# Writing an attention mask into the score banks from ScalarE instead of TensorE, in a kernel of attention and mixture of experts on one core

## The reference

```python
# layer 0: attention, 16 heads of 64, one key and value head for all
q = l2norm(ln(x) @ Wq) * q_scale ; k = l2norm(kv[..., :64]) * k_scale   # a null key and value in front
sim = einsum('bhid,bjd->bhij', q, k) * 8 + attn_bias                   # bias from relative positions
sim = where(causal, neg, sim)
sim = where(mask, sim, neg)                                            # mask: (16, 256), one bool per key
x = x + ln(einsum('bhij,bjd->bhid', softmax(sim), v) @ Wout) * g_out
# layer 1: router with top 2 of 8 experts, two shared experts, leaky gates
y = sum over chosen experts of weight * (leaky(x @ w_gate) * (x @ w_up)) @ w_down
x = x + y + shared experts
```

## Time and profile before

| | before |
|---|---|
| median of 3 executions | 1048.13 us (1047.93 to 1050.3) |
| profiled execution, its own time | 1048.86 us |
| its span (first to last instruction) | 1047.1 us |
| granted TensorE clock, mean | 0.997 |
| busy PE / DVE / ACT / POOL | 96% / 67% / 50% / 42% |
| 16 steps of one round (round 5, slot of step 0 to slot of step 15) | 649.44 to 717.52 us |

### The profile page before, as it was taken

One profiled execution on the slowest core, in us unless ns is written; L12 is line 12 of the kernel. 1 busy time (PEld: TensorE's weight loads), 2 busy tenths in 40 slices (PEclk: granted clock), 3 DMA queues, 4 the chain that ended last, 5 costly groups with the idle time before them and its releaser, 6 DMA issues.

```text
span 1047.1 us, 19955 instructions
## 1 busy us (share of the span) xinstructions
PE 1006.9 (96%) x6774; PEld 811.3 (77%) x6774; DVE 703.5 (67%) x2459; ACT 523.6 (50%) x1556; POOL 437.4 (42%) x422
## 2 busy tenths in 40 slices
PE   3878999999999999999999999999999999999998
PEld 2656977778777887778777797777877788777877
DVE  8887677765867558674777657676586755856553
ACT  3588256652566345662466615655256633565220
POOL 1645155443364344451545415454335434444212
PEclk9999999999999999999999999999999999999999
DMA  5220305121331112321132212321133111232042
GB/s 201 78 75 2 125 7 172 62 92 61 102 102 61 62 41 90 104 71 42 61 105 69 71 62 61 113 71 42 61 98 105 62 41 42 86 107 72 22 141 101
DMA packets 39539, 82.21 MB, mean 79 GB/s; under 512 B 4032, under 2 KB 18880, under 8 KB 39184
## 3 DMA queue, kind: packets, MB, share of 16 engines
q1 hardware_dynamic: 38480, 78.32, 22.8%
q10 hardware_dynamic: 960, 2.62, 0.7%
HBM read 71.33 MB, written 9.60 MB: 77 GB/s over the span
## 4 chain that ended last, share of the span: by engine, by line
PE 83%; DVE 8%; issue 2%; ACT 2%; DVEq 0%; POOL 0%
PE psY L1685 14%; PE psS L1552 7%; PE psG L70 6%; PE psG L72 6%; PE psG L71 6%; PE psO L1588 6%; PE psT L1563 5%; PE psS L1548 3%; PE psS L71 3%; PE psS L70 3%; PE psS L72 3%; PE psT L1570 2%; PE psO L1591 2%; PE psT L70 2%; PE psT L72 2%
## 5 line engine op out<-in xcount | busy, mean ns | idle before, releaser
L634 POOL TENSOR_TENSOR work<-work,rden 128x514 f32<-128x514 f32 x128 | 134.3, 1049 | 313.8 <-DVE rden L1179 313.8
L1685 PE MATMUL psY<-Wd,H 128*128 128x256 f32 x640 | 171.7, 397 | 0.0
L782 ACT ACTIVATE work<-work,low 128x257 f32<-128x257 f32 x256 | 128.3, 502 | 54.7 <-DVE low L1197 53.7
L70 PE MATMUL psG<-x1T_hi,Wgu 128*128 128x512 f32 (+1 forms) x292 | 134.7, 461 | 2.1 <-ACT leaky L826 1.9
L1685 PEld LDWEIGHTS psY<-Wd,H 128*128 128x128 f32 x640 | 111.7, 189 | 29.0 <-issue 14.6
L1197 DVE CUSTOM_DVE_ANT_0 work<-psS,bias,null_s 128x256 f32<-128x256 f32 x256 | 113.2, 479 | 24.3 <-PE psS L1552 22.8
L1293 DVE SCALAR_TENSOR_TENSOR leaky<-leaky 128x512 f32<-128x512 f32 x80 | 57.0, 713 | 103.2 <-ACT leaky L826 102.3
L623 POOL TENSOR_TENSOR rq<-qss,neghalf 128x16 f32<-128x16 f32 x32 | 97.6, 3050 | 43.8 <-DVE qss L1173 43.8
L72 PE MATMUL psG<-x1T_lo,Wgu 128*128 128x512 f32 (+1 forms) x292 | 114.5, 392 | 0.0
L71 PE MATMUL psG<-x1T_hi,Wgu 128*128 128x512 f32 (+1 forms) x292 | 114.0, 390 | 0.0
L1552 PE MATMUL psS<-KB,qT 64*128 64x256 f32 (+1 forms) x1024 | 105.8, 326 | 0.0
(11 more groups left out here) (262 smaller groups left out, 2288.9 us busy)
## 6 DMA issues: line engine op xcount, KB each, us to landing
Wgu<-wexp SPq DMA_DIRECT2D x70, 512.0 KB, 3.4
Wb<-wscr SPq DMA_DIRECT2D x64, 256.0 KB, 3.7
wexp<-Wgu SPq DMA_DIRECT2D x10, 512.0 KB, 3.3
xres<-in_x SPq DMA_DIRECT2D x8, 512.0 KB, 3.8
xin<-in_x SPq DMA_DIRECT2D x7, 512.0 KB, 4.5
out<-work SPq DMA_DIRECT2D x7, 512.0 KB, 3.0
raw<-in_wgu SPq DMA_DIRECT2D x10, 256.0 KB, 4.6
bias<-bscr SPq DMA_DIRECT2D x4, 512.0 KB, 5.9
```

Of the source, the lines that this page charges most:

```text
L70: te.matmul(dst, a_hi, b_hi, start=start, stop=False)
L634: pool.tensor_tensor(T1[sl][:, hs, :], T1[sl][:, hs, :], rden[sl][:, 1, hs].unsqueeze(2) .to_broadcast([P, 2, N + 1]), ALU.mult)
L782: act.activation(T1[sl][:, h, :], T1[sl][:, h, :], ACT.Exp, scale=-1.0, bias=low[sl][:, 1, h:h + 1], accum_out=den[sl][:, 1, h:h + 1])
L1685: mm = te.matmul(psY[:, t // 2, (t % 2) * D:(t % 2 + 1) * D], H[:, k % H_RING, t * P:(t + 1) * P], Wd[:, ORDER[k], :], start=(k == 0 and t ...
```

## The change

From round 1 on ("the second round"), for steps 1 to 15, TensorE's two mask matmuls go. In their place ScalarE writes the mask's terms of step n+1, one Copy of 2 x 384 columns from `MK` (bf16, SBUF) to both score banks (fp32, PSUM), between its two exponentials of 257 columns and its two of 129 columns in step n. TensorE's score of step n+1 then waits for this copy (`mask_ps`) in place of VectorE's two reads, and its products add to what stands in the banks. Step 0 of every round, and all of round 0, stay as they were. So that every partition has its mask, the load broadcasts it to all 128 partitions, with two DMAs in place of four.

```diff
--- before.py
+++ after.py
@@ -335,7 +335,7 @@
 
         xin_in = events("xin_in", 16)
         xres_in = events("xres_in", 16)
-        mask_in = events("mask_in", 64)
+        mask_in = events("mask_in", 32)
         wscr_in = events("wscr_in", 16, 16)
         wb_in = [events(f"wb_in{i}", 16 * (E // WB_RING)) for i in range(WB_RING)]
         out_in = events("out_in", 16, 16)
@@ -377,6 +377,7 @@
         qs_done = events("qs_done", TILES)
         qT_a = events("qT_a", TILES)
         exp_done = events("exp_done", GROUPS * STEPS)
+        mask_ps = events("mask_ps", ALL - 1)
         pt1_done = events("pt1_done", GROUPS * STEPS)
         x1T_a = events("x1T_a", KC)
         lex_done = events("lex_done", 1)
@@ -479,11 +480,10 @@
 
                 need(sp, mk_done, r - 1, 1)
                 stand(sp, waited_sp)
-                for i in range(2):
-                    for a, b in ((0, N), (N, P)):
-                        sp.dma_start(mask8[i * DH:i * DH + 1, :, a:a + b],
-                                     mask[:, bass.ds(r * TOK, TOK)].rearrange("a (b j) -> a b j", b=BB)[:, :, 0:b]) \
-                            .then_inc(mask_in.sem, 16)
+                for a, b in ((0, N), (N, P)):
+                    sp.dma_start(mask8[:, :, a:a + b],
+                                 mask[:, bass.ds(r * TOK, TOK)].rearrange("a (b j) -> a b j", b=BB)[:, :, 0:b]
+                                 .to_broadcast([P, BB, b])).then_inc(mask_in.sem, 16)
 
             def load_round(r):
                 load_mask(r)
@@ -756,7 +756,7 @@
                     if n >= VALUE_LAG:
                         head_out(r, n - VALUE_LAG)
                     if n < ALL:
-                        exps(r, n // STEPS, n % STEPS)
+                        exps(r, n // STEPS, n % STEPS, moe)
                     if moe is not None and n in GATE_AT:
                         take_gate(moe, GATE_AT[n])
                     if moe is None and 0 <= n - SPLIT_AT < W_RING:
@@ -774,7 +774,12 @@
                 act.activation(oT[0][:, STEPS * (g % 2) + s, (g // 2) * N:(g // 2 + 1) * N], value_bank(n)[:, 0:N],
                                ACT.Copy).then_inc(o_lead.sem, 1)
 
-            def exps(r, g, s):
+            def put_mask(r, n):
+
+                act.activation(psS[:, :, 0:N + P], MK[:, n // STEPS // 2, :].unsqueeze(1).to_broadcast([P, 2, N + P]),
+                               ACT.Copy).then_inc(mask_ps.sem, 1)
+
+            def exps(r, g, s, moe):
                 sl = g % 2
                 n = g * STEPS + s
                 need(act, s1_read, r, n + 1)
@@ -782,6 +787,8 @@
                     act.activation(T1[sl][:, h, :], T1[sl][:, h, :], ACT.Exp, scale=-1.0,
                                    bias=low[sl][:, 1, h:h + 1], accum_out=den[sl][:, 1, h:h + 1])
                 need(act, s0_read, r, n + 1)
+                if moe is not None and n + 1 < ALL:
+                    put_mask(r, n + 1)
                 for h in (2 * s, 2 * s + 1):
                     last = act.activation(T0[sl][:, h, :], T0[sl][:, h, :], ACT.Exp, scale=-1.0,
                                           bias=low[sl][:, 0, h:h + 1], accum_out=den[sl][:, 0, h:h + 1])
@@ -1032,7 +1039,7 @@
                     ins = dve.tensor_tensor(kd[:, :, i, :], kn[:], qk_scale[:].unsqueeze(1)
                                             .to_broadcast([P, TILES, DH]), ALU.mult)
                 ins.then_inc(kd_done.sem, 1)
-                need(dve, mask_in, r, 64)
+                need(dve, mask_in, r, 32)
                 dve.tensor_scalar(MK[:], mask8[:], -BIG, BIG, ALU.mult, ALU.add).then_inc(mk_done.sem, 1)
                 sum_q(r, 1)
                 if moe is not None:
@@ -1479,7 +1486,7 @@
                         need(te, qT_a, r, 2)
                         need(te, qT_v, r, 2)
                     if n < ALL:
-                        score(r, n // STEPS, n % STEPS)
+                        score(r, n // STEPS, n % STEPS, moe)
                     if n == VALUE_LAG and moe is not None:
 
                         need(te, wT_done, moe, 1)
@@ -1535,22 +1542,26 @@
                 if following is not None:
                     q_first(following)
 
-            def score(r, g, s):
+            def score(r, g, s, moe):
 
                 bb, p = g // 2, STEPS * (g % 2) + s
                 n = g * STEPS + s
                 q0 = bb * N
 
-                need(te, s1_read, r, n)
-                need(te, s0_read, r, n)
-                for i in range(2):
-                    half = slice(i * DH, (i + 1) * DH)
-                    te.matmul(psS[:, i, 0:N + P], pick_bf[half, :], MK[half, bb, :], start=True, stop=False)
+                added = moe is not None and n > 0
+                if not added:
+                    need(te, s1_read, r, n)
+                    need(te, s0_read, r, n)
+                    for i in range(2):
+                        half = slice(i * DH, (i + 1) * DH)
+                        te.matmul(psS[:, i, 0:N + P], pick_bf[half, :], MK[half, bb, :], start=True, stop=False)
+                else:
+                    need(te, mask_ps, moe, n)
                 for first, q1, keys_ in ((0, q0 + P, N), (N, q0, P)):
                     for i in range(2):
                         half = slice(i * DH, (i + 1) * DH)
                         mm = te.matmul(psS[:, i, first:first + keys_], qT[half, p, q1:q1 + P], KB[half, bb, 0:keys_],
-                                       start=False, stop=(first == N))
+                                       start=False, stop=(first == N or added), skip_group_check=added)
                 mm.then_inc(s_ps.sem, 1)
 
             def turn(r, n):
```

## The result

| | before | after |
|---|---|---|
| median | 1048.13 us | 1073.62 us (1071.67 to 1077.01, 4 executions) |
| ratio of the executions | | 1.0242, 95% interval 1.0208 to 1.0276 |
| profiled execution, span | 1048.86, 1047.1 us | 1071.79, 1070.0 us |
| granted clock, mean of the span | 0.997 | 0.994 |

A forecast was written before the change was run, and what follows sets the result against it. TensorE, busy 96% of the span, was taken as the bound. Late copies outweighed the removed pairs: five rounds 11.5 us, round 7 +0.3, round 1 +3.5, together +15.3, 1064.2 us; stated median 1063.5 us, range 1050 to 1075.

The forecast's parts named there:

- The copy's cost: ScalarE's 768-column copy: 0.80 us, ends 0.57 and 1.03; 0.92 us from its opening (copy start) to TensorE's score product.
- The carry through the gate's copy: A copy in a gate step pushes ScalarE's gate copy by 0.69 us, then VectorE's leak and scores, and the next opening.
- step 2: Score product at 658.20 against 656.75, 1.45 us late, because step 0's copy delays the gate's copy and the next opening.
- The normalisation at step 11: Gate step with 2.38 us of normalisation on VectorE behind `leak`; the next opening moves 1.55 us later, to 709.54.
- step 13: Round 5: copy ready at 710.46 against 707.81, score products 2.65 us late; the present 0.23 us wait is contained.
- s: How late a step's score products start against before; falls by 0.17 us a step where nobody waits.
- What the removal gives: TensorE: 105 pairs at 0.17 us, at most 17.9 us; bounds: nothing if the score's weight load replaces it, and 0.34.
- Rival B: Faster, 12%: copy 0.60 us (-13.2) and pair worth 0.27 us (-5.6), giving 1045.4 us.
- Rival D: Dearer, 12%: copy costs as the 1024-column row, 1079.4 us, or uncovered score weight load in steps without waits, 1073.7 us.
- Steps 10 and 11: VectorE comes late from step 8's statistics; s is 1.29 at step 10, 1.24 at step 11, losing most of its 0.17.
- Round 1: Also has splits (620 ns on ScalarE, six steps); 1.2 us added for about two without cover: +3.5 us.
- The mask's load: Two DMAs of 128 rows replace four of one, issued a round ahead of use; costed at nothing.

The follow-up runs named there:

- the spare copy into SBUF: The kernel before with all its pairs, plus 105 ScalarE copies of the same size and place into an unread SBUF tile: 1054.17 us, ratio 1.0052.
- the control: The kernel before with the next input's statistics moved to step 14 and its normalisation to step 17: 1059.25 us, ratio 1.0105.

## Why the prediction was right, and where its sizes were off

The sign, the mechanism and the places of the large losses were right, and the time lies in the range; the 25.5 us measured are 10 more than forecast. That it lies in the range is in part luck: the top of 1075 us was set for a dearer weight load, nothing in it stood for the clock, and one of the four executions came with 1075.4, one with 1077.0. Point by point:

- **The copy's cost.** 0.80 us were taken, 0.79 measured; TensorE followed 0.85 us after its start, 0.92 were taken. The ends 0.57 and 1.03 were not needed. The Trainium skill, "ScalarE: Activation LUTs", section "What ACT_TABLE_LOAD costs", gives 186 ns and 0.833 ns a column, which makes an estimate of 0.826 us for this size: the spare copy into SBUF took 0.829. Into PSUM it took 0.792, so the same page's rule that ScalarE reaches PSUM faster than SBUF (section "Step-by-step: what each stage is for") agrees with these runs, by 0.04 us.
- **The carry through the gate's copy.** Shown three ways: step 2 is 1.41 us late with all copies and 0.69 without the one in the gate step; the spare copies that nobody reads still delay step 2 by 0.39; and VectorE's wait for the gate's copy grew from 102.3 to 131.3 us.
- **The normalisation at step 11.** 1.58 us forecast for step 13 (s from 1.07 to 2.65), 1.54 measured, and gone when the normalisation is moved.
- **What the removal gives: mis-sized.** "I take 0.17, the start-to-start distance". The runs show 0.07: the lower bound named there, the score's own weight load coming into the open, is most of the truth. It matters where nobody waits. Apart from the clock, rounds 2 to 6 end 0.6 us later each than forecast, round 7 1.0, and each of the seven stretches between rounds 0.1, 4.7 us in all, after the small errors named here are set off. Rival B's 0.27 is excluded.
- **TensorE's clock: missing.** No term held it. In the profiled execution its falls at step 13 cost 2 x 1.6 = 3.2 us, and two of the other executions had a lower mean clock still. Rival D had the size of the result (it gave 1073.7 us for an uncovered weight load), but it put 0.17 on each of eight steps; about half of the missing 10 us came from there, most of the rest from the clock.
- **Steps 10 and 11: almost nothing.** The forecast let TensorE arrive 0.34 us less late at step 10 than at step 8, and then wait 0.14 for the copy. With 0.07 us a step it arrives only 0.14 less late, and by the forecast's own sum the copy is then ready 0.06 us ahead of it. So this is the mis-sized pair once more; it had put 0.26 us a round too much into the forecast at steps 10 and 11. Only the weight loads wait there (0.17 and 0.24 us in round 5).
- **Round 1**: +3.5 forecast, +3.8 measured. Most of what it loses beyond rounds 3 to 5 stands at step 10, where TensorE waits 0.48 us for the copy; with the statistics in step 14 that wait is gone. The mask's load, costed at nothing, cost nothing: the run with copies for steps 3, 7, 8, 9, 11, 14 and 15 has it too, and lands on its forecast. Round 0 was 0.5 us shorter, since the clock's falls in it stood elsewhere.

## What to carry to other kernels

Before work moves from the busiest engine to an idle one, lay the two timelines over each other: what counts is not the other engine's share of busy time but, step by step, when it reaches the new instruction and when the result is wanted, and what is queued behind that instruction. A new instruction ahead of one for which a third engine waits comes back a step later as a second delay; so place it only in the steps that have cover. Here that alone turned 2.4% of loss into 0.4% of gain, and together with the moved normalisation into 0.8%. Compare such a pair of edits with a kernel that has only one of them. And measure the removed work by leaving it out: a short matmul between others can be worth less than its distance, because it hides the next weight load.

## What the runs showed of the hardware

- TensorE's granted clock fell to half (1.2 GHz) at step 13 of the profiled executions behind an idle of 2.6 or 2.7 us in 6 of 6 rounds, of 1.8 us in 2 of 5, of 2.0 us in 0 of 1 and of 1.4 us in 0 of 6. Ahead of the idles at step 13 that a fall followed, TensorE had been busy for 10 us without another idle of 0.3 us. Behind the idle of 1.3 us at step 2 it never fell; behind one of 1.27 us at the end of the loop it fell in 4 of 6 rounds of the changed kernel with late statistics and in 0 of 6 of the control. At step 13 the longer idles were followed by a fall more often, but the length alone does not order the cases. A fall in rounds 1 to 7 cost about 1.6 us. What decides in which of several equal rounds it falls stays open.
- Two matmuls of 384 columns side by side on half the rows each took 0.17 us from start to start and were worth 0.07 when they were left out.
- A ScalarE copy of 768 columns from bf16 in SBUF took 0.792 us into two banks of PSUM and 0.829 us into SBUF.
- Waiting earlier on TensorE, with the semaphore long there, changed nothing (ratio 1.0000).
